# Routed expert tiles of 128 places instead of 256, with the token copy moved from VectorE to ScalarE

## The reference

```python
# L1_gnn: weights exp(e[j]) of the neighbours j of i, normalised
h = jnp.tanh(input @ W + b);  inp = input @ W;  e = (h @ a)[:, 0]
w = jnp.where(mask, jnp.exp(scores - m), 0.0)
out = (w / jnp.maximum(denom, 1e-30)) @ inp
# L1_ffn: every token goes to the K = 2 experts of E = 8 with the best gate
gate_scores = x @ Wg + bg
_, idx = jax.lax.top_k(gate_scores, K)
mask = jax.nn.one_hot(idx, E, dtype=x.dtype).sum(axis=-2)
h = jax.nn.gelu(einsum('td,edh->teh', xf, W1) + b1[None], approximate=False)   # H = 256
y = einsum('teh,ehd->ted', h, W2) + b2[None]
out = einsum('ted,te->td', y, mf)
```

## Time and profile before

| | |
|---|---|
| Median of 3 runs | 872.54 us (872.32 to 875.49) |
| Profiled execution | 872.16 us, of it the span of the trace 870.4 us |
| PE busy | 707.3 us (81% of the span) |
| DVE busy | 558.2 us (64%) |
| ACT busy | 477.4 us (55%) |
| POOL busy | 195.4 us (22%) |
| Attention and dense experts | until about 540 us |
| Graph gather of the third layer | about 580 to 720 us |
| Routed tiles | about 720 to 850 us |
| Outputs read back and stored | about 850 us to the end |

### The profile page before, as it was taken

One profiled execution on the slowest core, in us unless ns is written; L12 is line 12 of the kernel. 1 busy time (PEld: TensorE's weight loads), 2 busy tenths in 40 slices (PEclk: granted clock), 3 DMA queues, 4 the chain that ended last, 5 costly groups with the idle time before them and its releaser, 6 DMA issues. The chain is left out here.

```text
span 870.4 us, 11409 instructions
## 1 busy us (share of the span) xinstructions
PE 707.3 (81%) x3368; PEld 414.1 (48%) x3368; DVE 558.2 (64%) x1521; ACT 477.4 (55%) x704; POOL 195.4 (22%) x230
## 2 busy tenths in 40 slices
PE   1747999999999999999931895569999986877840
PEld 1643444444444444444421795435555545766740
DVE  7785668686767686767766267864556566544525
ACT  1746888888888888888842474131222323223310
POOL 2240000000000000000004421100355344677770
PEclk9979999999999999999965898679999996799985
DMA  4108999999989999887601000040011013233318
GB/s 128 71 1 243 304 256 270 254 261 258 265 260 256 270 243 281 242 256 223 185 7 31 1 0 0 8 121 1 26 35 38 29 40 80 62 99 97 92 47 289
DMA packets 101721, 122.56 MB, mean 141 GB/s; under 512 B 9230, under 2 KB 80146, under 8 KB 101664
## 3 DMA queue, kind: packets, MB, share of 16 engines
q1 hardware_dynamic: 96416, 113.02, 45.6%
q0 software_dynamic: 4544, 8.54, 3.0%
q10 hardware_dynamic: 704, 0.33, 0.1%
HBM read 86.56 MB, written 36.20 MB: 141 GB/s over the span
## 5 line engine op out<-in xcount | busy, mean ns | idle before, releaser
L528 DVE SCALAR_TENSOR_TENSOR probs<-adj,probs 128x1024 f32<-128x1024 int32 x128 | 156.7, 1224 | 105.4 <-ACT probs L501 98.5
L451 PE MATMUL ps<-x,qT 128*128 128x512 f16 x768 | 188.0, 382 | 3.2 <-PEq L186 3.2
L501 ACT ACTIVATE probs<-ps 128x1024 f32<-128x1024 f32 x128 | 131.0, 1023 | 51.2 <-PE ps L451 51.2
L512 ACT ACTIVATE mask<-probs 128x1024 fp8e4<-128x1024 f32 x128 | 134.0, 1047 | 0.0
L463 PE MATMUL ps<-probs,v 128*128 128x512 f32 x256 | 130.8, 593 | 0.0
L1285 PE MATMUL ps<-mask,parts 128*128 128x512 fp8e4 x512 | 116.3, 384 | 7.7 <-DVE parts L1550 7.7
L451 PEld LDWEIGHTS ps<-x,qT 128*128 128x128 f16 x768 | 75.4, 98 | 94.7 <-issue 5.6
L672 POOL TENSOR_TENSOR x<-x,beta 128x512 f32 x8 | 9.8, 1264 | 391.2 <-DVE xn L699 391.2
L534 DVE TENSOR_TENSOR p_lo<-probs,p_hi 128x512 f16<-128x512 f32 x128 | 87.6, 685 | 0.1
L1533 POOL DMA_INDIRECT mixed_spill<-mask,xn x78 | 77.3, 991 | 32.8 <-issue 21.8
L1486 POOL DMA_INDIRECT sorted_rows_spill<-rows,slots x64 | 63.0, 984 | 92.2 <-issue 54.7
(11 more groups left out here) (261 smaller groups left out, 905.1 us busy)
## 6 DMA issues: line engine op xcount, KB each, us to landing
adj<-in_adj SPq DMA_DIRECT2D x128, 512.0 KB, 5.2
sorted_rows_spill<-blank SPq DMA_DIRECT2D x32, 528.0 KB, 6.7
sorted_rows_spill<-blank SPq DMA_DIRECT2D x26, 198.0 KB, 7.5
xn<-sorted_rows_spill SPq DMA_DIRECT2D x39, 132.0 KB, 2.3
mask<-mixed_spill SPq DMA_DIRECT2D x8, 512.0 KB, 5.6
mask<-in_x SPq DMA_DIRECT2D x4, 512.0 KB, 5.8
feat_spill<-mask SPq DMA_DIRECT2D x8, 256.0 KB, 2.0
x_feat<-in_x SPq DMA_DIRECT2D x8, 256.0 KB, 4.8
```

Of the source, the lines that this page charges most:

```text
L451: ins = nc.tensor.matmul(out, qT[:, q_half, j], kT[:, c, k_half * GROUP:(k_half + 1) * GROUP], start=(n == 0), stop=(n == 2))
L501: nc.scalar.activation(probs[:, k % RING, :], ps[:, b:b + 2, :].rearrange("p b n -> p (b n)"), ACT.Exp, scale=1.0 / QK_SCALE ** 2).then_in ...
L512: nc.scalar.activation(mask[:, k * W:(k + 1) * W], probs[:, k % RING, :], ACT.Sign, saturate=False).then_inc(mask_kept, 1)
L528: nc.vector.scalar_tensor_tensor(out=probs[:, k % RING, :], in0=adj[:, k % LOADS, :], scalar=0.0, in1=probs[:, k % RING, :], op0=ALU.is_gt ...
```

## The change

Tiles become half as long: 128 places, 71 of them, of which 41 are in the early table. Each has one load, one transpose, one scatter; `up` has 128 columns in place of 256, `down` two matmuls in place of four. The copy of the tokens goes from DVE to ACT. There are four weight sets in place of three, and DVE fetches weights three tiles ahead, behind `keep_outputs`. In the graph part `turn` stands one group later in every chunk and the last `rank` one group earlier. At the hinge the gates of the last chunk stand ahead of the tile loop, its choice is made at step 0, its statistics used by ACT at step 0, its ranks at step 3, its scatters still at step 4, and the rest of the table at step 20 in place of 5. The arrays `passed` and `filled` lie in `values` now and are larger.

The core of the diff:

```diff
-ROUTED_STEPS = (2 * N + E * (2 * P - 1)) // (2 * P)
+ROUTED_STEPS = (2 * N + E * (P - 1)) // P
-EARLY = -(-(2 * GROUP * EARLY_CHUNKS - E * (2 * P - 1)) // (2 * P))
+EARLY = -(-(2 * GROUP * EARLY_CHUNKS - E * (P - 1)) // P)
-MOST_TILES = N // (2 * P)
+MOST_TILES = N // P
...
-        WEIGHTS = 3
+        WEIGHTS = 4
         current = room.take(WEIGHTS, EXPERT_WIDTH)
-        tokens = room.take(RING, 2 * P)
-        hT = room.take(SLOTS, FH, 2 * P)
-        y = room.take(LOADS, 2, D)
+        tokens = room.take(RING, P)
+        hT = room.take(SLOTS, FH, P)
+        y = room.take(LOADS, D)
         both = room.take(RING, 2, SUB, D)
-        sorted_rows = xn_room.take(LOADS, 2, ROW)
+        sorted_rows = xn_room.take(LOADS, ROW)
-        GATE_AT, CHOOSE_AT, STAGE_AT, RANK_AT, SCATTER_AT, TABLE_AT = 0, 1, 1, 2, 4, 5
-        part_of = lambda f: slice(f * 2 * P, (f + 1) * 2 * P)
+        CHOOSE_AT, STAGE_AT, RANK_AT, SCATTER_AT, TABLE_AT = 0, 0, 3, 4, 20
+        part_of = lambda f: slice(f * P, (f + 1) * P)
...
-                        sp.wait_ge(y_out[u], 32 * (k // LOADS))
-                    sp.dma_start(sorted_rows[:, u, :, :], io["sorted"][bass.ds(start, 2 * P), :].rearrange("(h p) n -> p h n", p=P))\
+                        sp.wait_ge(y_out[u], 16 * (k // LOADS))
+                    sp.dma_start(sorted_rows[:, u, :], io["sorted"][bass.ds(start, P), :])\
                         .then_inc(rows_in[u], 16)
...
-                            if c and g == 2:
+                            if c and g == 3:
                                 pe.wait_ge(rows_added, c)
...
-                            if c and g == 7:
+                            if c and g == (6 if c == LAST else 7):
                                 pe.wait_ge(chosen_ready, c)
...
-                    for h in range(2):
-                        ins = nc.tensor.transpose(ps[:, XT_BANK + k % 2, h * P:(h + 1) * P], sorted_rows[:, u, h, 0:D], sb["ident"][:, :])
-                    ins.then_inc(tile_turned, 1)
+                    nc.tensor.transpose(ps[:, XT_BANK + k % 2, 0:P], sorted_rows[:, u, 0:D], sb["ident"][:, :]).then_inc(tile_turned, 1)
...
                 up(0)
+                pe.wait_ge(last_xT, 1)
+                gate().then_inc(last_gates, 1)
                 for k in range(ROUTED_STEPS):
                     if k + 2 < ROUTED_STEPS:
                         turn_rows(k + 2)
                     if k + 1 < ROUTED_STEPS:
                         up(k + 1)
                     down(k)
...
+                def keep_tokens(k):
+                    act.wait_ge(tile_turned, k + 1)
+                    nc.scalar.activation(tokens[:, k % RING, :], ps[:, XT_BANK + k % 2, 0:P], ACT.Copy).then_inc(tokens_ready, 1)
+
+                act.wait_ge(last_added, 1)
+                keep_tokens(0)
+                keep_tokens(1)
                 act.wait_ge(last_turned, 1)
                 keep_turned().then_inc(last_xT, 1)
                 act.wait_ge(early_landed, count_)
                 act.sem_inc(moved_on, 1)
                 for k in range(ROUTED_STEPS):
+                    if k + 2 < ROUTED_STEPS:
+                        keep_tokens(k + 2)
                     gelus(k)
...
-                keep_tokens(1)
                 for k in range(ROUTED_STEPS):
-                    if k + 2 < ROUTED_STEPS:
-                        load_weights(k + 2)
-                        keep_tokens(k + 2)
                     keep_outputs(k)
+                    if k + WEIGHTS - 1 < ROUTED_STEPS:
+                        load_weights(k + WEIGHTS - 1)
```

More of the change, by code:

```diff
@@ L1028, in _ @@
                 ch.mark(nc.vector.tensor_scalar(place[:, :], place[:, :], float(N), None, ALU.mult))
-                ch.mark(nc.vector.tensor_scalar(sb["bound"][:, :], step[:, 0:MOST_TILES], float(2 * P), None, ALU.mult))
+                ch.mark(nc.vector.tensor_scalar(sb["bound"][:, :], step[:, 0:MOST_TILES], float(P), None, ALU.mult))
                 dve.wait_ge(gate_mean, 1)
@@ L1129, in gather_and_route @@
         count, ends, many, coef = (buf(n, [P, E]) for n in ("count", "ends_of", "many", "coef"))
[L1130 removed]
         ordered = buf("ordered", [P, E, E])
[L1132 to L1133 removed]
+        passed, filled = (values[:, u, :, :].rearrange("p s d -> p (s d)")[:, 0:n * E].rearrange("p (k e) -> p k e", k=k)
+                          for u, n, k in ((0, EARLY, EARLY), (1, MOST_TILES, E)))
+        expert_of, first = buf("expert_of", [P, max(EARLY, REST)]), buf("first", [P, max(EARLY, REST)])
         bound, used = sb["bound"], sb["used"]
@@ L1378, in down @@
                         pe.wait_ge(y_ready, k - 1)
-                    for h in range(2):
-                        for f in range(FH):
-                            ins = nc.tensor.matmul(ps[:, Y_BANK + k % 2, h * D:(h + 1) * D], hT[:, k % SLOTS, f, h * P:(h + 1) * P],
-                                                   current[:, k % WEIGHTS, F + f * D:F + (f + 1) * D], start=(f == 0), stop=(f == FH - 1))
+                    for f in range(FH):
+                        ins = nc.tensor.matmul(ps[:, Y_BANK + k % 2, 0:D], hT[:, k % SLOTS, f, :],
+                                               current[:, k % WEIGHTS, F + f * D:F + (f + 1) * D], start=(f == 0), stop=(f == FH - 1))
                     ins.then_inc(down_ready, 1)
@@ L1531, in _ @@
                     pool.wait_ge(y_ready, k + 1)
-                    for h in range(2):
-                        nc.gpsimd.indirect_dma_start(
-                            out=io["mixed"][:, :],
-                            out_offset=bass.IndirectOffsetOnAxis(ap=sorted_rows[:, u, h, D:D + 1].bitcast(U32), axis=0),
-                            in_=y[:, u, h, :], in_offset=None, bounds_check=2 * N - 1, oob_is_err=False).then_inc(y_out[u], 16)
+                    nc.gpsimd.indirect_dma_start(
+                        out=io["mixed"][:, :],
+                        out_offset=bass.IndirectOffsetOnAxis(ap=sorted_rows[:, u, D:D + 1].bitcast(U32), axis=0),
+                        in_=y[:, u, :], in_offset=None, bounds_check=2 * N - 1, oob_is_err=False).then_inc(y_out[u], 16)
             @block.vector
@@ L1631, in tile_starts @@
                         ch.link(nc.vector.tensor_scalar(first[:, 0:n], first[:, 0:n], at_, None, ALU.add))
-                    ch.link(nc.vector.scalar_tensor_tensor(out=first[:, 0:n], in0=step[:, 0:n], scalar=float(2 * P), in1=first[:, 0:n],
+                    ch.link(nc.vector.scalar_tensor_tensor(out=first[:, 0:n], in0=step[:, 0:n], scalar=float(P), in1=first[:, 0:n],
                                                            op0=ALU.mult, op1=ALU.add))
@@ L1636, in early_tiles @@
                 def early_tiles(ch):
-                    ch.link(nc.vector.scalar_tensor_tensor(out=filled[:, :, :], in0=count[:, :].unsqueeze(2).to_broadcast([P, E, MOST_TILES]), scalar=float(2 * P - 1),
+                    ch.link(nc.vector.scalar_tensor_tensor(out=filled[:, :, :], in0=count[:, :].unsqueeze(2).to_broadcast([P, E, MOST_TILES]), scalar=float(P - 1),
                                                            in1=bound[:, :].unsqueeze(1).to_broadcast([P, E, MOST_TILES]), op0=ALU.subtract, op1=ALU.is_gt))
                     ch.link(nc.vector.tensor_reduce(many[:, :], filled[:, :, :], AX.X, ALU.add))
-                    ch.mark(nc.vector.tensor_scalar(coef[:, :], many[:, :], float(-2 * P), float(N), ALU.mult, ALU.add))
+                    ch.mark(nc.vector.tensor_scalar(coef[:, :], many[:, :], float(-P), float(N), ALU.mult, ALU.add))
                     rank_experts(ch)
```

28 lines of the change are left out of this document (10 added, 18 removed).

## The result

The changed kernel takes 887.28 us (median of 6 runs, 885.92 to 890.77), the kernel before 873.25 beside it (6 runs). The ratio is 1.0161, 95% interval 1.0131 to 1.0191. I forecast 886.7, so the sign and the size are right. The profiled execution took 885.92 us, with a span of 884.1.

What follows compares the result with a forecast made beforehand. POOL's scatters bound the tile part before; afterwards a PE-ACT circle of 1.72 us a tile would. The last landing moves from 849.56 to 863.8, +14.2 on the profiled 872.16; with 0.4 for the median 886.7 us, range 868 to 901.

Steps and rivals of the forecast that it cites:

- The circle: Tile loop: transpose, ACT's copy, two Gelus, `down`, next transpose wait on each other and set the pace, ahead of POOL's 1.30.
- Its size, 1.72: Tile loop, us a tile: ACT 0.80, PE 0.88, PE's end to ACT's start 0.04; bounds 1.55 to 1.94.
- The graph part, net -1.0: Before the tile loop: later `turn` saves 2.1 us, larger table operations cost 1.1.
- The hinge: Graph part to tile loop: last chunk's scatters start at 737.3, not 747.34; tile 12's rows come at 753.1, PE stands 7 us.
- 58 circles: Tile loop from tile 12 to the transpose of tile 70, at 1.72 us each: 99.8 us.
- the clock: After PE's wait for tile 12: some 4 us at 1.2 GHz stretch two turns of the loop, +1.2 us.
- the table: Rest of the table at step 20, in the open: 4.8 us of work delays `down(23)` by 3.5 us (0 to 4.1).
- The tail: After tile 70's transpose: 1.2 to `down(68)`, 1.8 for two tiles, then 0.7 + 0.4 + 2.1 to the last landing.
- Rival 1: Tile loop: POOL stays the bound, kernel gets faster, 858.5 us; chance 0.14 including loop steps between 1.30 and 1.48.
- Rival 2: Tile loop: a step near 1.5 us because queues hide fixed times, loss and gain cancel, 868 to 876 us; chance 0.10.
- Rival 3: Tile loop: TensorE falls to 1.2 GHz, +0.55 us a tile, +32 us, 919 us; chance 0.06.

Runs made afterwards that it cites:

- opened circle: Changed kernel with ACT's two Gelus of tile k put ahead of its copy of tile k+2: 899.63 us, ratio 0.9985 to the kernel before.
- graph-only run: Kernel before with only the graph-part moves (transposes one group later, last rank one group earlier): 906.86 us, ratio 1.0039.

## Why the prediction was right

- *The circle sets the loop.* Shown. Each wait of it stands in the trace, one Gelu less makes it 1.44, and with the Gelus first it opens: 1.31 a tile where loads are in stock.
- *Its size, 1.72.* Measured 1.70: from the copy's start to the last Gelu's end 0.79 (0.80 forecast), from there to the transpose's end 0.87 (0.88), PE's end to ACT's start 0.04 (0.04). Copy and Gelu take 277 and 365 ns, as taken from the slope. The Trainium skill (ScalarE: Activation LUTs, section What ACT_TABLE_LOAD costs) would have the copy at 293 and the circle at 1.80; here the measurement decides against it.
- *The graph part, net -1.0.* The last chunk's transposes came at 716.70 instead of 720.22, -3.5. The table's long operations took 0.49 us instead of 0.30 each, as forecast; PE's idle time fell by 2.3. Three traces with the change have these transposes at 716.7 to 718.6, three without at 719.4 to 722.3, all on the chips with the shorter time: about -3 on average, with 2 to 3 us between traces of the same part. The term was too small by some 2 us. Which part gave it wasn't tried on such a chip.
- *The hinge.* From the statistics to the slots 10.8 us (10.7 forecast). The statistics are 3.0 us early, from the term before; POOL takes up the slots 0.9 us after they are ready, which had no term, so the scatters start at 735.27, 2.0 early. Tile 4's scatter follows 10.46 later (10.4), its issue and landing took 2.4 (3.0), the load 1.95 (2.4). So tile 12's transpose is at 750.08 instead of 753.1.
- *58 circles, the clock, the table.* From that transpose to the one of tile 70 (855.52) it is 105.4 us, 104.5 forecast. 58 x 1.70 = 98.6, the table +4.0 (5.73 less a period; +3.5 forecast), and 2.8 are left for the clock against 1.2 (by its own figures, two circles of five records of 0.109, it is 1.1). The clock is the term that was too small: it fell a second time, behind the table's stall. The intervals of 2.10, 2.32 and 2.08 there are 1.4 us over.
- *The tail.* From tile 70's transpose to the landing at 863.13 it is 7.6 us, 6.2 forecast. Up to the last `down`, at 858.54, it is 3.0 as forecast, and DVE has added its bias at 859.58:

```profile
859.29 0.29 DVE L1679 TENSOR_TENSOR mask<-ps,mask 128x128 f32<-128x128 f32 x1 [0.69 <-PE ps L1378]
```

But POOL issues the scatters of tiles 68 and 69 until 860.74 (858.50 and 859.77, 0.97 each) and comes to the last one at 861.05, 1.4 us after the 859.64 that the forecast's 0.7 + 0.4 give. The sum had let POOL be free there: without copies the last tiles come closer than its 1.28 us.
- *Sum.* 3.0 less, then 0.9 and 1.4 more: the last landing at 863.13, forecast 863.8. That the total is only 0.6 us off is luck in part: terms of 3.0 and 2.3 us nearly cancel. The median lay 1.4 us above the profiled execution, not 0.4.

Rival 1 (POOL stays the bound) fell with the circle at 1.70; its pace, 1.28 to 1.31, is that of the opened circle on the third chip. Rival 2 (a circle near 1.5, with queues that hide fixed times) fell by the same number. Rival 3 fell: the clock is 1.00 in the loop, behind the two stands alone it is less. The 73% that rival 3 gives for PE before is 75% by its own record of 0.109 us (18 in 2.60); nothing hung on it.

What stays open: why PE's signals are late on two chips, in the loop over 256 rows as well. The runs that should tell were made on a chip without it. How many records or signals PE has in a us can't be the whole of it: the graph-only run has 4.0 records a us from 760 to 860 us, as many as from 100 to 400, and in the graph gather of the changed kernel on the second chip (640 to 720 us) only 9 of 22 signals, 0.3 a us, have their update in time. Also open is the time of the opened circle on a chip like that of the result; it wasn't run there without another edit. The copy on ACT gained 0.6% with 256 rows, and the whole change lost 1.6%. The difference fits the halved tile with its fixed parts: from tile 4 on 67 x 1.70 = 114 us against 35 x 2.60 = 91.

## What to carry to other kernels

When a step is moved to another engine, write down the circle that it closes: who waits for whom until the first is reached again. Its length a turn competes with the busiest engine's, and halving the tile doesn't halve it. Put the work that only others wait for (Gelus of k) ahead of the work for two steps on (copy of k+2).

A gain read on one chip need not be there on another: take the changed kernel along in each group of runs.

## What I had not expected of the hardware

- On two of three chips the time of the kernel before is 901 to 902.5 us instead of 874, with a mean granted clock of 0.894 to 0.909 instead of 0.910 to 0.920. There, from 760 to 860 us, between 26 of 87 and 69 of 149 signals of PE have their update within 0.06 us of the product's end, on the third all but one at most. Some updates are only missing from the trace; what readers see is fewer: signals that come 1.4 to 2.6 us late, every 5 to 10 us in the opened loop and in that over 256 rows, and 8.0 in the worst place (graph-only run, a product that ends at 772.79 and the Gelu at 780.79). Up to 575 us, with some 4 records a us, all are in time on each chip.
- A new instruction starts on ACT about 0.1 us before the last one ends, on PE 0.11 to 0.17 (fences above), so a chain inside one engine is shorter than the sum of its durations.
- SP needs about 1.1 us for one load whose address it reads from a table, and 0.06 for an increment.
